# Attention over causal key tiles: the 384 and the 128 wide diagonal tile of a row block in one group

## What is computed

```
h = _rmsnorm(x, norm_w)                       # 8 batches, 1024 rows, 128 wide
q = (h @ Wq)  -> 4 heads of 32;   k, v = (h @ Wk), (h @ Wv) -> 2 heads of 32, repeated
q = _l2norm(q);  k = _l2norm(k)
attn = jnp.einsum('bhqd,bhkd->bhqk', q, k) * exp(log_temperature)
attn = jnp.where(causal, attn, -jnp.inf)
attn = jax.nn.softmax(attn, axis=-1)
out = jnp.einsum('bhqk,bhkd->bhqd', attn, v) ... @ Wo
return x + gate * out
```

## Time and profile before

| | us |
|---|---|
| median of 3 runs (lowest, highest) | 459.21 (459.12, 459.47) |
| time of the profiled execution | 459.42 |
| span of its trace | 457.6 |
| PE busy | 413.5 |
| ACT busy | 382.8 |
| DVE busy | 354.2 |
| POOL busy | 260.6 |

### The profile page before, as it was taken

The page is one execution under the profiler, slowest core; times in us unless marked ns, Lnnn a source line. Parts: engine busy times, 40 slices in busy tenths (PEclk is TensorE's granted clock), DMA queues, the critical chain, the costliest instruction groups (busy, mean ns, idle before and its releaser), DMA issues.

```text
span 457.6 us, 10470 instructions
## 1 busy us (share of the span) xinstructions
PE 413.5 (90%) x3747; PEld 214.1 (47%) x3747; DVE 354.2 (77%) x872; ACT 382.8 (84%) x546; POOL 260.6 (57%) x321
## 2 busy tenths in 40 slices
PE   0779998989998999999999999999999998999995
PEld 0346665663334335335335335345344244767554
DVE  5899997799499789689689689687647937878654
ACT  3799999667968988988988988988977998999961
POOL 5499999973444444444453553541131456998951
PEclk9999999999999999999999999999999999999999
DMA  5586433334026072084072072092070112557462
GB/s 161 127 163 149 65 53 69 70 71 96 20 53 134 1 140 48 1 140 47 0 138 46 0 138 47 1 139 48 1 139 0 24 26 49 136 93 139 93 116 74
DMA packets 119151, 34.94 MB, mean 76 GB/s; under 512 B 101569, under 2 KB 119105, under 8 KB 119105
## 3 DMA queue, kind: packets, MB, share of 16 engines
q1 hardware_dynamic: 117824, 34.02, 38.9%
q10 hardware_dynamic: 1280, 0.33, 0.3%
HBM read 4.98 MB, written 4.19 MB: 20 GB/s over the span
## 4 chain that ended last, share of the span: by engine, by line
PE 51%; issue 14%; ACT 12%; DVE 11%; POOL 7%; DMA 2%; DVEq 0%; SPq 0%; POOLq 0%; ACTq 0%
PE ps L507 11%; PE ps L706 11%; PE ps L687 9%; PE ps L711 9%; ACT XN L458 4%; PE ps L558 3%; PE ps L569 3%; ACT PT L817 3%; PE ps L594 2%; DVE H L327 2%; ACT SG L476 2%; DVE X L1021 2%; PE ps L691 2%; POOL OL L281 2%; DVE AN L1008 1%
## 5 line engine op out<-in xcount | busy, mean ns | idle before, releaser
L817 ACT ACTIVATE PT<-ps,k_exp 128x1024 f32<-128x1024 f32 (+1 forms) x192 | 162.0, 899 | 20.2 <-PE ps L691 14.8
L507 PE MATMUL ps<-XT,WT 128*128 128x512 f16 x384 | 95.0, 386 | 8.6 <-DVE H L327 3.1
L687 PE MATMUL ps<-QKT 128*128 128x512 f16 (+3 forms) x384 | 87.1, 328 | 11.4 <-ACT PT L817 9.3
L706 PE MATMUL ps<-PT,V 128*32 128x512 f32 (+3 forms) x768 | 81.8, 498 | 0.0
L711 PE MATMUL ps<-PT,ones 128*32 128x512 f32 (+3 forms) x768 | 79.6, 486 | 0.0
L433 POOL TENSOR_TENSOR HL<-H,HH 128x1024 f16<-128x1024 f32 x31 | 67.0, 2160 | 7.3 <-ACT HH L482 5.1
L327 DVE SCALAR_TENSOR_TENSOR H<-SG,k_isilu,ps 128x1536 f32<-128x1536 f32 x32 | 58.0, 1811 | 14.9 <-ACT SG L476 5.6
L281 POOL TENSOR_TENSOR OL<-ON,OH 128x512 f16<-128x512 f32 x15 | 18.2, 1216 | 77.4 <-ACT OH L277 77.4
L687 PEld LDWEIGHTS ps<-QKT 128*128 128x128 f16 x384 | 27.8, 97 | 69.2 <-ACT PT L817 60.1
L507 PEld LDWEIGHTS ps<-XT,WT 128*128 128x128 f16 x384 | 34.6, 99 | 54.1 <-issue 14.5
L458 ACT ACTIVATE XN<-X,NB,RS 128x128 f32<-128x128 f32 x128 | 52.4, 482 | 2.7 <-POOL NB L405 2.7
(11 more groups left out here) (139 smaller groups left out, 645.3 us busy)
## 6 DMA issues: line engine op xcount, KB each, us to landing
result<-X SPq DMA_DIRECT2D x15, 256.0 KB, 2.5
X<-in_L_attn_x SPq DMA_DIRECT2D x7, 512.0 KB, 4.5
X<-in_L_attn_x SPq DMA_DIRECT2D x2, 256.0 KB, 4.9
XT<-w_int SPq DMA_TRANSPOSE x32, 3.1
AXT<-AS SPq DMA_TRANSPOSE x16, 2.8
QKT<-ST SPq DMA_TRANSPOSE x16, 5.6
w_int<-in_L_ffn_w_gate SPq DMA_DIRECT2D x1, 192.0 KB, 4.3
w_int<-in_L_ffn_w_up SPq DMA_DIRECT2D x1, 192.0 KB, 4.5
```

What stands on the lines that cost most here:

```text
L507: i = e.matmul(out[:, j, :], WT[:, wp, w * NJ + j, :], XT[k % 2][:, xp, :], start=a == 0, stop=a == len(passes) - 1)
L687: i_ = e.matmul(o, QKT[k % 2][:, i // TPC, NH + hp, i % TPC * P:(i % TPC + 1) * P], QKT[k % 2][:, qc, 2 * hp + h, CH - n:CH], start=True, ...
L706: e.matmul(PVD[HD * h:HD * h + HD, 0, CH - n:CH], V[k % 2][:, i, v0:v0 + HD], PT[g % 2][:, h, 0:n], start=i == 0, stop=done, skip_group_ch ...
L817: e.activation(PT[g % 2][:, 2 * hp:2 * hp + 2, 0:n], SCORES[hp][:, :, 0:n], ACT.Exp, scale=k_exp[:, 0:1]).then_inc(a_exp, 1)
```

## The change

The tiles that are 384 and 128 wide, (qc, 4qc+1) and (qc, 4qc+3), become one group of 512 columns: the 384 wide one in columns 0 to 383 of the banks and of `PT`, the 128 wide one in 384 to 511. The 256 wide tile comes after it, on its own. Each row block has one group fewer (three for block 0, seven for block 1), so a batch has ten. All matmuls stay as they were in number and size; the exps of the two tiles are one instruction per head pair in place of two.

The uses are placed anew: `qkv` still after groups 0 and 1, `wo` 1 after group 2 (before: 3), `wo` 0 after group 9, the last (before: 10 of 0 to 11). On ACT, `o_hi` of the row block before goes after the exps of group 2 (before: of group 3), both `x_hi` go to the end of the batch, after the exps of the next batch's first group (before: one after the exps of group 10 and one after those of 11), and `HEAD` and `stack_hi` move one group number down. The diff without the lines that only follow from it:

```diff
-        groups = [(qc, i) for qc in range(QCS) for i in range(TPC * (qc + 1))]
+        def row_groups(qc):
+            d = TPC * qc
+            return [[(i, 0, CH)] for i in range(d + 1)] + \
+                [[(d + 1, 0, 3 * P), (d + 3, 3 * P, P)], [(d + 2, 0, 2 * P)]]
+
+        groups = [(qc, tiles_) for qc in range(QCS) for tiles_ in row_groups(qc)]
         NG = len(groups)
-        G0 = TPC
+        G0 = len(row_groups(0))
...
         USES = {0: [("qkv", 0, 0), ("qkv", 0, 1)], 1: [("qkv", 1, 0), ("qkv", 1, 1)],
-                3: [("wo", 1)], 8: [("rows", 0)], 10: [("wo", 0)], 11: [("rows", 1)]}
+                2: [("wo", 1)], 7: [("rows", 0)], 9: [("wo", 0), ("rows", 1)]}
 
-        MOVED = {0: [], 1: [], 3: USES[0], 4: USES[1]}
+        MOVED = {0: [], 1: [], 2: USES[0], 3: USES[1]}
...
+                for i, o, n in tiles_:
                     for h in range(2):
-                        i_ = e.matmul(SCORES[hp][:, h, 0:P], ident16[:, :], causal[:, :], start=False,
-                                      stop=True, skip_group_check=True)
+                        i_ = e.matmul(SCORES[hp][:, h, o:o + n],
+                                      QKT[k % 2][:, i // TPC, NH + hp, i % TPC * P:(i % TPC + 1) * P],
+                                      QKT[k % 2][:, qc, 2 * hp + h, CH - n:CH], start=True, stop=True,
+                                      skip_group_check=o > 0)
+                    if i >= TPC * qc:
+                        for h in range(2):
+                            i_ = e.matmul(SCORES[hp][:, h, o:o + P], ident16[:, :], causal[:, :], start=False,
+                                          stop=True, skip_group_check=True)
                 i_.then_inc(a_s, 1)
...
-            HEAD = {5: 0, 6: 1, 8: 2}
+            HEAD = {4: 0, 5: 1, 7: 2}
...
-                    if g == 2 and k >= 1:
+                    if g == 1 and k >= 1:
                         o_hi(e, b * 2 - 1)
                     if g == 8:
                         o_hi(e, b * 2)
...
-                        g_ = g - 3 if k == 0 else g
+                        g_ = g - 2 if k == 0 else g
                         if g_ in (0, 1):
                             qkv_out(k + 1, m0 + g_, k, b, g_)
                         g_ = g - 2 if k == 0 else g
-                        if g_ in (5, 6):
-                            stack_hi(m0 + (g_ == 6), int(g_ == 6))
-                    if k + 2 < B and g in (9, 10):
-                        x_hi(m0 + 2 + (g == 10), int(g == 10))
+                        if g_ in (4, 5):
+                            stack_hi(m0 + (g_ == 5), int(g_ == 5))
+                    if k + 2 < B and g == NG - 1:
+                        x_hi(m0 + 2, 0)
+                        x_hi(m0 + 3, 1)
```

More of the change, by code:

```diff
@@ L630, in uses_in @@
                 us = MOVED.get(g, USES.get(g, [])) if k == 0 else USES.get(g, [])
-                if k == B - 1 and g >= NG - 2:
-                    us = USES[10] if g == NG - 1 else []
                 return planned([u for u in us if not (u[0] != "wo" and k == B - 1)
@@ L669, in width @@
         def width(g):
-            qc, i = groups[g]
-            return CH - max(0, i - TPC * qc) * P
+            return sum(n for _, _, n in groups[g][1])
         def att_pe(e, shift, first=None, head=None):
@@ L676, in scores @@
             def scores(k, b, g, hp):
-                qc, i = groups[g]
-                n = width(g)
+                qc, tiles_ = groups[g]
                 G = b * NG + g
@@ L681, in scores @@
                     e.wait_ge(a_exp, 2 * G + hp - 1)
-                if hp == 0 and i == 0:
+                if hp == 0 and tiles_[0][0] == 0:
                     e.wait_ge((d_u if shift else d_t)[qc], b * 16 + 16)
[L684 to L688, removed]
@@ L689, in scores @@
-                if diag:
-                    for h in range(2):
-                        i_ = e.matmul(SCORES[hp][:, h, 0:P], ident16[:, :], causal[:, :], start=False,
-                                      stop=True, skip_group_check=True)
+                for i, o, n in tiles_:
+                    for h in range(2):
+                        i_ = e.matmul(SCORES[hp][:, h, o:o + n],
[6 more added lines that the diff above has]
+                                          stop=True, skip_group_check=True)
@@ L693, in scores @@
                 i_.then_inc(a_s, 1)
             def weigh(k, b, g):
-                qc, i = groups[g]
-                n = width(g)
+                qc, tiles_ = groups[g]
                 G = b * NG + g
                 e.wait_ge(a_exp, 2 * G + 2)
-                again = i == 0 and k * QCS + qc >= 1
+                again = tiles_[0][0] == 0 and k * QCS + qc >= 1
                 if again:
                     e.wait_ge(a_pvc, 2 * (b * QCS + qc) - 1)
[L703 to L707, removed]
+                for i, o, n in tiles_:
+                    for h in range(NH):
+                        v0 = DQ + DK + HD * (h // 2)
+                        e.matmul(PVD[HD * h:HD * h + HD, 0, CH - n:CH], V[k % 2][:, i, v0:v0 + HD],
+                                 PT[g % 2][:, h, o:o + n], start=i == 0, stop=i >= TPC * qc,
+                                 skip_group_check=True)
@@ L708, in weigh @@
                 if again:
                     e.wait_ge(a_pvc, 2 * (b * QCS + qc))
[L710 to L713, removed]
+                for i, o, n in tiles_:
+                    for h in range(NH):
+                        i_ = e.matmul(PVD[HD * h:HD * h + HD, 1, CH - n:CH], ones32[:, :],
+                                      PT[g % 2][:, h, o:o + n], start=i == 0, stop=i >= TPC * qc,
+                                      skip_group_check=True)
@@ L794, in step @@
                             use(None, None, u)
-                    if k == 0 and g == 3:
+                    if k == 0 and g == 2:
                         e.wait_ge(s_res, NC)
```

## The result

The changed kernel takes 462.07 us (median of 4, 461.83 to 463.67), the kernel before in the same session 459.3 (4 executions, 459.12 to 459.47). The ratio is 1.0069, with a 95% interval of 1.0053 to 1.0085: **slower by 0.7%, 2.8 us**, where 457.0 and a small gain had been forecast, and outside the range of 454.8 to 459.8.

A forecast was written before the change was run, and what follows sets the result against it. PE and ACT were both taken as near full, so their waits count. Batch 0 +0.1, batches 1 to 5 -0.65, batch 6 -0.45 and the last -1.3 sum to -2.3 us, giving 457.0 us, range 454.8 to 459.8.

The forecast's parts named there:

- The unit: On PE, 512 columns of matmul cost 0.21 us; a full group has 12 of them.
- the fixed 0.27 a group: On PE, each group costs 0.27 us beyond its columns, where PE changes width; two groups fewer save 0.54 a batch.
- the seams inside a group: On PE, each joined group has two more seams inside weigh at 0.03 us each, 0.12 a batch.
- rival 4: PE's fixed cost goes by tile, not group: 0.06 us a batch saved instead of 0.42, kernel 459.9; 6%.
- The border wait: Between batches, with the casts late, PE waits 0.31 us for `PVS` and 1.23 for AXT.
- rival 1: PE's border wait isn't there: a batch takes 1.23 us less, kernel 449.6; 6%.
- The stall left inside: Inside the batch, scores of (1,1) wait behind exps of (1,0) on ACT: 0.8 us, bounds 0.3 and 1.5.
- The end: Last batch, first to last PV about 26.5 us; the second feed-forward moves with it, together 1.3 us saved.
- the three stalls: In the kernel before, beside narrow groups, PE waits for ACT 0.70, 0.54 and 0.81 us, 2.05 a batch.
- The step that failed: DVE at the border: wo_out 1.5 us later, ON about 6.9 after PV(0,0), ACT asking at about 7.3, so covered.
- rival 3: About no change: 0.2 to 0.5 us more at a border, or the inside stall at 1.5: 458.3 to 460.1; 16%.
- Rival 2: Border wait longer and kernel slower: from 0.52 us a border over 460.1, at 1.0 a border 463.0; 12%.

The follow-up runs named there:

- experiment 4: Kernel before, twelve groups, with both AS casts moved to the border behind the exps of the next batch's first group: 471.22 us, ratio 1.0265.
- Experiment 5: Changed kernel with POOL's x_lo cut to one tile of four from batch 1's inputs on: 455.55 us, ratio 0.9934 to the kernel before.
- experiment 1: Changed kernel with add_norm ahead of wo_out of `wo` 0 on DVE: 456.18 us, ratio 0.9942 to the kernel before.
- experiment 3: Changed kernel with add_norm ahead of `wo` 0 on DVE and the AS casts at groups 8 and 9: 449.21 us, ratio 0.9775 to the kernel before.
- experiment 2: Changed kernel with the AS casts early again, at groups 8 and 9, DVE unchanged: 456.22 us, ratio 0.9939 to the kernel before.
- experiment 8: Repeat of the changed kernel with add_norm ahead of `wo` 0 and AS casts at groups 8 and 9: 448.83 us, ratio 0.9785 to the kernel before.

## Why the prediction was wrong

**Right, and confirmed term by term.** The unit and the fixed 0.27 a group: the turns of 14 and 13 units are 3.28 and 3.06, 0.02 or 0.03 over the sum, so the seams inside a group cost nearly nothing (0.12 a batch had been set down) and rival 4 falls. The border wait: AXT 1.04 where 1.23 was walked, PVS 0.17 to 0.26 for 0.31 (0.45 at the first border); experiment 4 shows it in the old groups, and rival 1 falls. The stall left inside was put at 0.8; with DVE's lateness removed it is 0.9 (3.40 against 11 units, 2.98 against 12) and the batch 33.81 for 33.83, so the sum of these terms holds, to 0.02 by some luck, since single terms are off by 0.1 to 0.2 either way. The end:

```profile
352.17 1.07 PE L708 MATMUL ps<-PT,V 128*32 128x512 f32 x8
...
378.66 0.64 PE L708 MATMUL ps<-PT,V 128*32 128x256 f32 x8
...
381.23 1.02 PE L507 MATMUL ps<-XT,WT 128*128 128x512 f16 x4 [0.73 <-DVE PVS L249]
```

First to last PV of the last batch is 26.49 (26.5 forecast), and from that first PV to the second feed-forward it is 29.06 against 30.42 before: -1.36 for -1.3. Batch 0 went from 35.23 to 34.87, -0.36 for +0.1, but in an execution whose clock did not fall; the other three have a lower mean clock (0.994 to 0.996 for 0.999), and what their batch 0 took is not known.

One reading of the working is wrong without consequence. Of the three stalls "in which PE waits for ACT", that of (0,3) to (1,0) is a wait of 0.45 for POOL's `OL`, at 221.73, ahead of `wo` 1.

**The step that failed** is "DVE's wo_out now comes at the border, 1.5 us later than now, and after it come add_norm, stats, the reciprocal (3.3) and ON, about 6.9 after PV(0,0)", and ACT asking at about 7.3: "covered, by a small 0.4". ACT asked at 7.2, `ON` was ready at 8.08 (220.86 - 212.78). The figures of the walk fit an add_norm of 2.3, its length in the kernel before; with 2.3 in place of 3.56 `ON` would have been ready at 6.8, and the 0.4 would have been there. That length comes from a place that only the last 0.4 us of one x_lo touches, and was used where the same change had put two. Experiment 5 shows it from the other side: short x_lo, 2.24. What it cost is 1.0 in each of batches 1 to 5, as experiment 1 measures: 0.89 and 0.43 of waits on ACT, then 1.01 on PE. Five batches of it are 5.0, and 462.07 is 5.1 above the forecast. That these agree so well is partly luck: the start of the attention alone differs by up to 1.2 us between the profiles (first PV at 106.97 to 108.15), and the execution of 462.07 is not the profiled one.

The same loss can be read as a term of the sum: the stall inside the batch, put at 0.80, was 1.9 (4.40 against 11 units, 2.98 against 12). Its stated upper bound was 1.5. And that bound, at the prediction's own +4.2, gives 461.2, which rival 3 lists under 458.3 to 460.1 and the range leaves out: the range was narrower than its own terms.

The Trainium skill has the rule ("SBUF — State Buffer", SBUF: two separate sides): GpSimd and a VectorE operation in a two-port mode share a pair of ports under an exclusive lock; whichever starts first has it for its whole instruction, and the other is blocked. The trace agrees: the add_norm instruction beside an x_lo of 1.16 us ends 0.08 or 0.09 us behind the x_lo's end, at 0.91 and 1.20 us instead of 0.33. That add_norm runs in such a mode, and the stats and the reciprocal do not, no run here tests; the traces show that it is slowed and they are not.

**Rival 2** had the sign, "the wait is longer and the kernel slower", from 0.52 a border on, and it named "DVE's ON has only 0.4" as its weak place. It was priced as a longer way to AXT; that way was not longer. So its 463.0 for 1.0 us a border came close to 462.07 with the right size and another cause. The prediction's own signs of it were both seen: batches over 34.4, and OH waiting for ON. It should have had more than 12%: a slack of 0.4 us on a chain of 20 DVE instructions behind a border on which the change moves two POOL instructions is no cover.

**What the profiled execution adds.** It was the slowest of the four, 463.67. In its batch 6 the transfer to AXT took longer:

```profile
321.75 1.47 PE L741 MATMUL ps<-QKVO,AXT 128*128 128x256 f16 x12 [2.67 <-DMA AXT<-AS]
...
DMA to landing us min/median/max: 3.9/4.1/4.3
```

4.3 instead of 2.7, and PE waits 2.67 in place of 1.04. Such transfers are not new. The kernel before has two at the border of batches 2 and 3 (tile AXT, 203 to 212 us):

```profile
DMA to landing us min/median/max: 3.7/4.2/4.7
```

There the batch took its 33.98 all the same, since the transfer had 5.9 us. The prediction read its 2.7 at one border only the earlier trace rows. Without slack a late first half is paid in full. The other three executions are 1.4 to 1.8 us shorter, which fits one such event; as their clocks differ too, more cannot be said.

## What to carry to other kernels

When a change moves an operation, move its neighbours' durations too: read the duration of an instruction beside the work it will have next to it, above all for DVE beside POOL, and give a slack that is smaller than one POOL instruction no credit. The same goes for a transfer: look at all its landings, not at one. An instruction that waits for the last event of a stage should stand behind everything on its queue that is ready, not ahead of it (one swap on DVE: 5.6 us here, each kernel taken against the one before of its session, and nothing where there was slack). And a merge of narrow tiles can be worth 1.6 us a batch and still lose, so measure it apart from the placing that comes with it.

## What was not expected of the hardware

Eight such DVE instructions with nothing beside them take 2.13 us (the normalisation of the changed kernel at 205.31). add_norm's eight took 2.24 beside two short x_lo (0.95 together), 2.71 beside one x_lo (1.16), 3.05 beside `OL` (1.27), 3.56 beside two x_lo (2.27), and 3.97 in experiment 3 beside `OL` and an x_lo (1.26 and 1.22). In each case but the short ones it is one instruction of the eight for each POOL instruction that is long, 0.91 to 1.26 us instead of 0.33, and it ends 0.08 to 0.09 behind the POOL instruction; the rest keep their length. POOL's instructions stay at 1.16 to 1.27. Stats and reciprocal beside an x_lo keep theirs too. The granted clock fell to 0.50 for 3.4 us (6.8 in experiment 2) in or behind a PE wait of about 3 us in four profiles (experiments 1, 2, 3, 5) and did not in two others with a wait of the same length (3.03 in the changed kernel, 3.04 in experiment 8); what decides it is open.
